# A two-layer decoder: the cross-attention and routing chain between attention and experts is cut into two halves of tokens

## What is computed

```python
x = norm(x + attention(x))              # 16 heads of 128, 4 key and value heads, causal, rotary
s = (x @ A) @ ctx.T                     # cross attention, 256 x 256 per batch
p = softmax(layer_norm(s) * gamma + beta)
x = norm(x + p)
logits = x @ w_router                   # 16 experts, the best 4 are kept, softmax over them
x = norm(x + shared_experts(x) + sum of gate[e] * expert[e](x))
expert(x) = (silu(x @ we1) * (x @ we3)) @ we2    # 16 of them, and 4 shared pieces alike
```

## Time and profile before

| | |
|---|---|
| median of 3 runs | 971.85 us |
| the profiled execution, its own time | 972.34 us |
| its span, from first to last instruction | 970.6 us |
| TensorE busy | 888.1 us (92%) |
| VectorE, ScalarE, POOL busy | 674.3, 410.8, 492.3 us |
| granted TensorE clock, mean | 0.965 of full |

### The profile page before, as it was taken

The page is one execution under the profiler, slowest core; times in us unless marked ns, Lnnn a source line. Parts: engine busy times, 40 slices in busy tenths (PEclk is TensorE's granted clock), DMA queues, the critical chain, the costliest instruction groups (busy, mean ns, idle before and its releaser), DMA issues. The chain is left out here.

```text
span 970.6 us, 15802 instructions
## 1 busy us (share of the span) xinstructions
PE 888.1 (92%) x4982; PEld 750.7 (77%) x4982; DVE 674.3 (69%) x1869; ACT 410.8 (42%) x1173; POOL 492.3 (51%) x399
## 2 busy tenths in 40 slices
PE   7889999999998669999968999999997689999995
PEld 5678888888887557777746888888886468888885
DVE  3696786786685679888876677677673755555555
ACT  4263553554565121111025666566664632223222
POOL 4766665755511242223335665555550238777773
PEclk8999999999999779999989999999999889999998
DMA  6221121122000331221000111101100001111111
GB/s 185 66 87 38 51 87 49 40 88 73 15 23 1 107 111 48 67 71 31 1 27 1 49 51 49 49 1 50 50 23 18 17 12 53 45 49 49 49 38 44
DMA packets 48106, 47.58 MB, mean 49 GB/s; under 512 B 4833, under 2 KB 39601, under 8 KB 48049
## 3 DMA queue, kind: packets, MB, share of 16 engines
q1 hardware_dynamic: 48048, 46.87, 15.5%
HBM read 45.81 MB, written 1.05 MB: 48 GB/s over the span
## 5 line engine op out<-in xcount | busy, mean ns | idle before, releaser
L826 ACT ACTIVATE a_probs<-bank,a_neg_peak 128x128 f32<-128x128 f32 (+1 forms) x256 | 103.4, 430 | 90.3 <-DVE a_neg_peak L934 90.3
L1390 DVE SCALAR_TENSOR_TENSOR b_acc<-bank,b_gate,b_acc 128x256 f32<-128x256 f32 x256 | 111.5, 479 | 14.0 <-PE bank L1301 8.0
L1300 PE MATMUL bank<-b_w,xt_hi 128*128 128x512 f32 x256 | 103.2, 403 | 1.5 <-DVE b_acc L1390 1.4
L1301 PE MATMUL bank<-b_w,xt_lo 128*128 128x512 f32 x256 | 101.6, 397 | 0.0
L854 ACT ACTIVATE a_probs<-a_probs,a_row_inv 128x128 f32<-128x128 f32 (+1 forms) x256 | 91.9, 447 | 19.0 <-DVE a_row_inv L942 19.0
L934 DVE CUSTOM_DVE_ANT_0 bank<-bank,causal 128x128 f32<-128x128 f32 (+1 forms) x256 | 82.4, 394 | 15.6 <-PE bank L696 15.2
L832 ACT ACTIVATE a_probs_t<-bank 128x512 f32<-128x512 f32 x96 | 53.9, 596 | 77.0 <-PE bank L716 77.0
L1505 POOL TENSOR_TENSOR d_h_lo<-d_h,d_h_hi 128x512 fp32r<-128x512 f32 x40 | 51.8, 1297 | 52.7 <-ACT d_h_hi L1624 39.2
L1710 DVE TENSOR_TENSOR d_h<-d_silu,bank 128x512 f32<-128x512 f32 x40 | 27.5, 688 | 73.0 <-PE bank L113 72.9
L735 PE MATMUL bank<-a_probs_t,a_vals 128*128 128x256 f32 x256 | 76.5, 380 | 0.0
L1258 POOL TENSOR_TENSOR b_masked<-b_raw,tern 128x1024 bf16<-128x1024 f32 x16 | 34.3, 2150 | 81.4 <-PE bank L1289 81.4
(11 more groups left out here) (267 smaller groups left out, 2575.7 us busy)
## 6 DMA issues: line engine op xcount, KB each, us to landing
b_raw<-_L_ffn_expert_masks_dram SPq DMA_DIRECT2D x32, 256.0 KB, 2.9
d_raw<-in_L_ffn_we_dram SPq DMA_DIRECT2D x48, 128.0 KB, 2.2
a_raw_k<-in_L_attn_w_k_dram SPq DMA_DIRECT2D x8, 512.0 KB, 6.5
a_raw_q<-in_L_attn_w_q_dram SPq DMA_DIRECT2D x8, 512.0 KB, 5.7
a_raw_v<-in_L_attn_w_v_dram SPq DMA_DIRECT2D x8, 512.0 KB, 7.3
a_raw_o<-in_L_attn_w_o_dram SPq DMA_DIRECT2D x8, 512.0 KB, 3.6
a_raw_q<-in_L_attn_Wq_dram SPq DMA_DIRECT2D x8, 512.0 KB, 4.6
a_raw_o<-in_L_attn_Wo_dram SPq DMA_DIRECT2D x8, 512.0 KB, 3.6
```

The lines of the kernel that those rows point to most:

```text
L826: nc.scalar.activation(probs[s % 2][:, i, at:at + width], c.banks[i][:, at:at + width], ACT.Exp, bias=neg_peak[:, n:n + 1], scale=-1.0, ac ...
L1300: nc.tensor.matmul(out, c.xt_hi[:, k, cols], w[j][:, k], start=k == 0, stop=False)
L1301: last = nc.tensor.matmul(out, c.xt_lo[:, k, cols], w[j][:, k], start=False, stop=k == KC - 1)
L1390: last = nc.vector.scalar_tensor_tensor(acc[e][:, t], c.banks[t % RING][:, e * D:(e + 1) * D], g, acc[e][:, t], ALU.mult, ALU.add)
```

## The change

- The chain between attention and experts becomes a class `Cross`, each of whose pieces works on one half. Its buffers for scores and probabilities hold a half.
- Half 0's pieces are put into steps 8 to 15 of the second attention, one or two a step, in each engine's list; their PSUM units join the ring (`CROSS_UNITS`). `hand_over` is VectorE's release of such a unit.
- Half 1's pieces are put into the experts' block, at units 0 to 12, on banks 6 and 7 (`CHAIN`).
- The experts go by units: a unit is one piece of weights for one half. The order is pieces 0 to 11 for half 0, the same 12 for half 1 with the weights kept, then pieces 12 to 19 for half 0 and for half 1: 40 units. The list is written out, without loops.
- The high part of expert weights is made by ScalarE in one copy of 768 columns, the low part by POOL (pieces 0 and 1 wholly by POOL, in step 14 of the attention).
- Down products have one pair of banks up to unit 11, then two pairs in turn. `keep_warm` of the old chain is gone.
- The second value buffer is gone; the values of half 1 are computed behind step 7 instead of 6. Three pieces of expert weights are loaded at the attention's start.
- Normalisations 5 and 6 take bn_stats moments on VectorE instead of sums on the way, a mean on POOL and squares on ScalarE; the negated maximum is one instruction. The last normalisation goes in parts of 4, 2 and 2 tiles.
- Layer 0's blocks call the same helpers by halves, in the order they had.

```diff
+CROSS_UNITS = {9: ("turned4", 0, 2), 10: ("attended", 0, 1), 11: ("similar", 0, 2), 12: ("weighted", 0, 2), 14: ("turned5", 0, 2), 15: ("logits", 0, 1)}
 # attention, POOL, in step s
+                    if rope and s == 8:
+                        cross.norm4.root(pool, HALF_TILES[0], 1)
                     if s % STEPS:
                         split_o(s // STEPS)
+                    if rope and s == 11:
+                        cross.similar_pool(pool, 0)
+                    if rope and s == 13:
+                        cross.norm5.root(pool, HALF_TILES[0], 1)
                     if s + 3 <= LAST:
                         split_proj(s + 3)
                     if s + 2 <= LAST:
                         rotate(s + 2)
...
+                    if rope and s == 14:
+                        for p in range(moe.EARLY):
+                            moe.hi_pool(pool, p)
+                            moe.lo_pool(pool, p)
 # attention, TensorE: behind scores(s + 1)
+                    if rope:
+                        cross_step(s)
...
-                    if rope and s == PASS_STEPS - 2:
+                    if rope and s == PASS_STEPS - 1:
                         values(1)
 # attention, ScalarE
+                    if rope:
+                        cross_step(s)
                     if s < LAST and not late:
                         exps(s + 1)
                     pt(s)
...
+                    if rope and s == 12:
+                        cross.exps_act(act, 0)
                     if s < LAST:
                         norm(s + 1)
 # attention, VectorE
+                    if rope and s == 8:
+                        dve.drain()
+                        cross.norm4.moments(dve, HALF_TILES[0])
                     if s < LAST:
                         peaks(s + 1)
+                    if rope:
+                        cross_step(s)
...
                     pv(s)
+                    elif rope and s == 8:
+                        cross.norm4.apply(dve, HALF_TILES[0], 1, cross.s_norm4)
+                    elif rope and s == 12:
+                        cross.add_dve(dve, 0)
+                    elif rope and s == 13:
+                        dve.drain()
+                        cross.norm5.moments(dve, HALF_TILES[0])
...
+                    if rope and s == 13:
+                        cross.norm5.apply(dve, HALF_TILES[0], 1, cross.s_norm5)
 # experts, POOL
+            cross.norm4.root(pool, HALF_TILES[1], 2)
+            for p in range(moe.EARLY, 4):
+                moe.lo_pool(pool, p)
+            for n in range(UNITS):
+                low(n)
+                if n == 3:
+                    cross.similar_pool(pool, 1)
+                elif n == 6:
+                    cross.norm5.root(pool, HALF_TILES[1], 2)
...
+                p = n + 4 if n < SLOTS else n - 1
+                if n < SLOTS - 4 or SLOTS < n <= PIECES:
+                    moe.lo_pool(pool, p)
 # experts, TensorE: chain(n) is half 1's piece
+            up(0)
+            up(1)
+            for n in range(UNITS):
+                if n + 2 < UNITS:
+                    up(n + 2)
+                chain(n)
+                down(n)
 # experts, ScalarE
+            nc.scalar.activation(primed[:], c.one[:], ACT.Silu)
+            for p in range(moe.EARLY, 4):
+                moe.hi_act(act, p)
...
+            for n in range(UNITS):
+                if n + 2 < UNITS:
+                    gate(n + 2)
+                chain(n)
+                if n + 2 < UNITS:
+                    high(n + 2)
+                p = n + 4 if n < SLOTS else n - 1
+                if n < SLOTS - 4 or SLOTS < n <= PIECES:
+                    if p >= SLOTS:
+                        act.wait_ge(s_out, 2 * unit_of[p - SLOTS, 1] + 2)
+                    moe.hi_act(act, p)
 # experts, VectorE
+            cross.gate_dve(dve, 0)
+            cross.norm4.moments(dve, HALF_TILES[1])
+            mult(0)
+            mult(1)
+            for n in range(UNITS):
+                if n + 2 < UNITS:
+                    mult(n + 2)
+                chain(n)
+                if n + 1 < UNITS:
+                    add(n)
```

More of the change, by code:

```diff
@@ L477, in ring_bank, with cross_banks @@
         return c.banks[5 + number[step, s, u] % RING]
+    def cross_banks(s):
+        step, half, count = CROSS_UNITS[s]
+        return [ring_bank(step, half, u) for u in range(count)]
     def taken(step, s, u):
@@ L1108, in root, with apply @@
         last.then_inc(self.s_rstd, 1)
[L1110 to L1120 removed]
+    def apply(self, dve, tiles, n, s_done):
+        dve.wait_ge(self.s_rstd, n)
+        for t in tiles:
             x = self.c.x[:, t]
             mean, op = (self.neg_mean[:, t:t + 1], ALU.add) if self.summed else (self.mv[:, t, 0:1], ALU.subtract)
[L1123 removed]
+            last = self.nc.vector.tensor_scalar(x, x, mean, self.rstd[:, t:t + 1], op, ALU.mult)
+        last.then_inc(s_done, 1)
 class Transposed:
@@ new lines, in raw_pe, with flat_act @@
+    def raw_pe(self, pe, turned, half, bank):
+        turned.wait(pe, half)
+        cols = slice(half * HALF, (half + 1) * HALF)
+        for k in range(KC):
+            w = self.w[:, k].rearrange("p r h e -> p (r h e)")
+            self.nc.tensor.matmul(bank[:], w, self.c.xt_hi[:, k, cols], start=k == 0, stop=False)
+            last = self.nc.tensor.matmul(bank[:], w, self.c.xt_lo[:, k, cols], start=False, stop=k == KC - 1)
+        last.then_inc(self.s_raw, 1)
+    def flat_act(self, act, half, bank):
+        act.wait_ge(self.s_raw, half + 1)
+        self.nc.scalar.activation(self.flat[:, half % self.halves], bank[0:2 * self.experts], ACT.Copy).then_inc(self.s_flat, 1)
@@ L1246, in _ @@
                 pool.sem_inc(s_masked, 2)
-                norm1.roots(pool, c.one_less)
+                for half in range(2):
+                    norm1.root(pool, HALF_TILES[half], half + 1, factor=c.one_less)
                 for x in acc:
@@ L1250, in _ @@
                 last.then_inc(s_acc0, 1)
-                norm2.roots(pool)
+                for half in range(2):
+                    norm2.root(pool, HALF_TILES[half], half + 1)
                 def mask(i, j):
@@ L1266, in _ @@
                 summed(nc.gpsimd, pool, 0).then_inc(s_sum, 1)
-                norm3.means(pool)
-                norm3.roots(pool)
+                for half in range(2):
+                    norm3.mean(pool, HALF_TILES[half], half + 1)
+                for half in range(2):
+                    norm3.root(pool, HALF_TILES[half], half + 1, squares=D)
             @block.tensor
@@ L1321, in _ @@
                 act.sem_inc(s_w, 2)
-                turned2.act(act)
-                router.act(act)
+                for half in range(2):
+                    turned2.act(act, half, turn_banks(half))
+                for half in range(2):
+                    router.flat_act(act, half, c.banks[half])
                 act.wait_ge(s_above, 1)
```

865 lines of the change are left out of this document (486 added, 379 removed).

## The result

The changed kernel takes 969.13 us (median of 20 runs) where the kernel before, in the same company, takes 972.46 (20 runs). The ratio is 0.9967, 95% interval 0.9955 to 0.9979: faster by 3.3 us, 2.0 to 4.4. Run again beside other kernels it took 968.34 (9 runs), ratio 0.9944 (0.9926 to 0.9962). One run of a kernel in a while is an outlier of 1.1 to 3 ms; the medians do not feel them.

A forecast was written before the change was run, and what follows sets the result against it. TensorE alone bounds the experts; in the second attention VectorE and POOL follow closely. Savings -42.9, moved products +12.9, attention waits +13.5, expert waits +12.6, clock +1.0 give -2.9 us: 969 us, range 963 to 975.

The forecast's parts named there:

- step 9, with its products: Second attention: POOL's splits hold VectorE's four applications of norm 4, so the turn comes 2.5 us later, bounds 0.2 and 5.
- step 14: Second attention: POOL's early pieces hold norm 5's applications, delaying the last output 4.3 us beyond the turn's products.
- the block of 40.24: Serial chain between attention and experts, 749.10 to 789.34, expected to go whole: 40.24 us saved.
- What goes: Savings: the stretch between attention and experts 40.24, first nine expert products 1.64, the kernel's end 1.0; sum 42.9 us.
- forecast mark of 768.5: Where TensorE's first expert product was expected to stand in the profile: about 768.5.
- POOL in VectorE's way: Second attention, steps 9 and 14: POOL holds VectorE's applications; waits in the attention sum to 13.5 us, without this 6.7.
- Low parts in the steady units: Experts, units 13 to 20: every second unit waits 1.41 us for POOL's low part, four times, 5.6 us.
- First units: Experts, units 0 to 12: waits of 7.0 us in all, among them 3.1 and 1.9 at units 6 and 7.
- the count that would have made 970.4: Experts, unit 5: by the skill's count of a drain at table switches, some 1.4 us more, sum 970.4.
- Clock: TensorE at half clock behind the waits at step 14 and unit 6: 1.0 us more, bounds 0 to 3.5.
- Rival 1: The chain hides as meant: waits at steps 9 and 14 and in the experts are gone, 955 us; chance 0.22.
- Rival 2: Experts: weights' split longer by d, some 14 splitting units each pay d/2; far end d 1.4, 979 us; chance 0.2.

The follow-up runs named there:

- e4: Changed kernel with VectorE's applications of norms 4 and 5 also writing an unused sum of each row, POOL's order unchanged: 964.56 us, ratio 0.9916.
- e3: Changed kernel with POOL waiting in step 9 for VectorE's application of norm 4 before it splits wo: 965.88 us, ratio 0.9925.
- e2: Changed kernel with POOL splitting the two early weight pieces behind step 15's split of wo, which waits for norm 5's application: 963.72 us, ratio 0.9913.
- e1: Changed kernel with ScalarE, in the experts, making the weights' high part ahead of its silu and the unit's high part: 964.33 us, ratio 0.993.
- e7: Changed kernel with ScalarE making the high part of pieces 12 to 19 in six instructions of 128 columns: 969.39 us, ratio 0.9967.
- e6: Changed kernel with the edits of e1 and e2 and three moves in POOL's and VectorE's order in the experts' first units: 951.63 us, ratio 0.9778.
- a_again: The changed kernel run once more, unedited, in other company: 968.34 us, ratio 0.9944.
- after_pad32: Changed kernel with 32 unused bytes a partition of SBUF reserved ahead of the second attention's weights: 970.37 us in a single execution.
- after_pad96: Changed kernel with 96 unused bytes a partition of SBUF reserved ahead of the second attention's weights: 970.55 us in a single execution.
- e8: As e6, with ScalarE in place of VectorE applying norm 4 to half 0 in step 9: 952.35 us, ratio 0.9803.

## Why the prediction was right, and where it was not

By its own steps, in the profiled executions:

| step of the prediction | forecast | measured |
|---|---|---|
| steps 0 to 5, over before | 0 | 0.6 |
| steps 6 and 7 with the values | 0.7 | 1.4 |
| step 8 | 1.2 | 1.0 |
| step 9, with its products | 3.65 | 3.0 |
| steps 10 and 11 | 3.0 | 2.6 |
| steps 12 and 13 | 4.85 | 5.1 |
| step 14 | 5.15 | 6.4 |
| last output to first expert product | 0.9 | 1.1 |
| first expert product to end of last `up` | 185.8 | 186.8 |
| behind that | 13.3 | 13.0 |
| sum of these, less the block of 40.24 | -2.9 | -0.5 |
| ahead of the first step of the second attention | 0 | -5.2 |

- *What goes.* Right: the block is gone whole, and the first expert product stands at 765.10. Counted as in the kernel before that is 770.26 (5.16 later, by the start of the attention's first step), 1.8 behind the forecast mark of 768.5.
- *POOL in VectorE's way.* Right in place and nearly in size: 4.87 and 6.63 for four applications against 4.3 and 6.6, waits of 2.3 and 4.0 against 2.5 and 4. Taking the hold away gave back 2.67 and 5.36 (e4), the order of POOL's list 1.4 and 5.35 (e3, e2). The forecast for both together was 6.8. The rule of the Trainium skill that the prediction leaned on (SBUF — State Buffer, "SBUF: two separate sides", an exclusive lock for a whole instruction) agrees with the plain form, one of POOL's instructions for each of VectorE's. The same section of the Trainium skill limits the lock to VectorE instructions in a two-port performance mode or with two inputs in SBUF; here the form with row sums took 0.54 each and was not held, and no run shows in which mode either form ran.
- *Step 14* is the largest miss in the attention, 1.3 more than forecast. e2 places it: the wait was 4.2 where 4.3 stood in the sum, and the half clock behind it took 1.2 more. The prediction had named that clock, but in its own term.
- *Low parts in the steady units.* Right: four waits of 1.3 where I had 1.41, in every second of the splitting units. ScalarE's 768 columns took 0.83 and POOL's 1.85, against 0.85 and 1.83. e1 shows that the order is the cause, e7 that the length counts once in a pair.
- *First units.* 3.25 and 1.8 us for units 6 and 7, against 3.1 and 1.9. The two table loads around the exponentials (800.65 and 805.30) took 1.28 each with the next instruction right behind, as in the earlier trace rows; no drain, so the count that would have made 970.4 falls again.
- *Clock.* 1.0 forecast, 2.5 measured: 1.2 at step 14, and 1.3 behind the wait of unit 6, where the twelve down products took 2.73 us, not 1.44. Both places were named; the size was too small, within its bounds of 0 to 3.5. The last output was at half clock as before.
- *Rival 1* was the measure of what could be had: 955. The waits it had to have gone were all there, e6 took most of them out by order alone, and got 951.6. Its premise, that they would hide by themselves, was false.
- *Rival 2.* Its far end was summed too high: the sizes that it names (1.26 us for 0.85, and 2.4 for 1.83) make d 1.0 and the time 976, not 1.4 and 979. No measured size came near them.
- *What failed.* Two things that nearly cancel, and that they do is luck. The terms behind the start of the second attention's first step sum to -0.5 in the profiled pair and not to -2.9; step 14 and the experts were 1.3 and 1.0 too short in the forecast, the others up to 0.7 off to either side. And the early part, which I put at nothing because its instructions are the same, is 1.44 us faster in seven eighths of the masked experts, some 1.65 in all, because the new classes reserve their buffers ahead of it. The other 3.5 of the 5.16 are chance of one execution: 1.7 in the first 35 us, 1.6 in a stretch of half clock between the second attention's first scores and its first step (11.63 us against 9.99; a_again has 11.69). Of the 3.3 us between the medians 1.65 are thus the placement, an estimate from the stretch, and 1.7 are left for the change itself. The single executions with other placements fit that: after_pad32 and after_pad96 took 970.37 and 970.55, against 972.11 for the kernel before beside them. But from execution to execution the part behind the start of the first step varies by more: it takes 445.8, 448.1 and 445.3 us in three profiles of the old instruction lists, 445.2, 446.1, 446.4 and 447.0 in four of the new, on average 446.4 and 446.2. With the 5.4 us between the medians of a_again and its company, less 1.65, the change itself brings between nothing and some 4 us; how much stays open. That it brings little until its waits are ordered away is shown.

## What to carry to other kernels

When idle time of a serial chain is filled by moving the chain between other work, the gain depends on a handful of instructions in in-order queues: list, for each wait of the bounding engine, the one instruction that stands ahead of the awaited one, move that, and see in the next profile whether the wait went or only moved. Here five such moves were worth some 17 us, the restructuring itself at most some 4. Reserve nothing ahead of a tuned stage without looking at that stage's own length in the profile again.

## What the runs showed of the hardware

- POOL's two-input instructions hold VectorE's plain tensor-scalar with both sides in SBUF, one for one (1.38 us for four became 4.87 and 6.63), but not its form with row sums (1.93 for four) and not its maxima on PSUM (256 columns took 0.46 to 0.47 us each, beside POOL and apart from it). They also hold an addition with two inputs in SBUF: the probabilities of half 1 beside POOL's `m_w_lo` took 3.22, where four with POOL idle took 1.67 (e1).

```profile
804.31 3.22 DVE L1653 SCALAR_TENSOR_TENSOR x<-d_probs,d_row_inv,x 128x256 f32<-128x256 f32 x4
...
805.36 1.89 POOL L1753 TENSOR_TENSOR m_w_lo<-m_raw,m_w_hi 128x768 fp32r<-128x768 f32 x1 [4.34 <-ACT m_w_hi L1749]
```

- Thirty-two unused bytes of SBUF made a stretch of 94.3 us take 95.8, with TensorE busy throughout in both. I had not expected any dependence of products on where their buffers stand.
- Behind one and the same wait TensorE's clock falls in one execution and not in the next: step 9 with its wait of 2.3 has 20.0 to 20.2 us in a_again, e2 and e6, with two microseconds at 0.50 in the middle, and 19.0 at 1.00 throughout in the changed kernel's first execution, e1 and e7. Where the wait is taken away (e3, e4) or down to 1.1 (e8) it stays at 1.00. A single profiled pair can't price an edit below that; lengths of stages without such a stretch can.
